# Edge filters as products over 32-row strips read back from memory, and image 0's first maxima ahead of the later filters

## The chip, the cores and the metric

One of the eight cores of a Trainium2 chip runs the whole program: TensorE (PE; PEld is its weight load), VectorE (DVE), ScalarE (ACT), GpSimd (POOL), and SyncE (SP), which issues most of the DMAs. The metric is the device time of one execution in microseconds.

## What is computed

A small two-layer "early fusion" model over eight images of 256 x 256 pixels and a text of 128 rows for each. The change concerns its first step only:

```python
w = (0.2989, 0.587, 0.114)
gray = einsum('bchw,c->bhw', x, w)                # x: 8 x 3 x 256 x 256, float32
edges = conv(gray, scharr, padding='SAME')        # two 3x3 filters
edge = abs(edges).sum(over the two filters) / 2   # 8 x 256 x 256
h = concat(edge, txt)                             # 8 x 384 x 256, 384 rows of 256 channels
```

Behind it stand layer 0 (normalisation, attention with 16 heads of 16 channels and two kinds of keys, whose softmaxes are mixed by alpha; then a feed-forward with blockwise 4-bit rounding) and layer 1 (attention over 64 anchors, then one shared and eight routed experts). All of it starts from `h`.

## The kernel before

All engines have instruction streams of their own, written out by hand, and wait on each other by semaphores. `attention0` holds the edge filters and layer 0's attention. Its attention runs as eight "turns", one an image (`for_images`, `turn`). A turn computes exponentials of scores of image i; beside them it prepares image i + 1's row maxima (`ring`) and image i + 2's projections. What the first turn needs has to be there before it: this part is the prologue, and the change lies in it wholly.

The prologue before, by engine:

- **SP** loads the pixels (`image(i)`, three DMAs of 256 KB, two buffers), weights, text, and the filters' taps. Then it stores the three bf16 parts of image 0's projections to DRAM (`store_parts(0)`, L374), reads them back as stacks of 16 partitions (`stacks`, L385; half 0 serves maxima 0 to 47, half 1 the rest), does the same for image 1 up to its first half, and writes the negated maxima of image 0 next to the queries (`maxima`, L394).
- **DVE** builds the filters' band matrices, makes gray rows of all eight images from the pixels (`make_gray`, L1083 and L1086), sums the two magnitudes into `h` (`edge_rows`, L1091), takes the moments of the three 128-row tiles of an image (`moments`, L1097, L1100), normalises images 0 and 1 (`inputs`, L939), computes the low parts of the projections (L950), and takes the 96 row maxima of image 0 (`ring`, L961) and their negation (L965, L968).
- **PE** computes the filters (`edges(i, n)`, L688, L692): a filter is three products with a banded 128 x 128 matrix over both 128-row halves of an image, 512 columns, and a fourth over six single rows that reach across the halves. Those rows are moved from partition to partition by two small DMAs an image, issued by ACT (`sides`, L860). Images 0 to 5 are filtered ahead of the ring, images 6 and 7 in pieces between its steps (`edge_piece`). PE also turns weights and inputs (L702, L550), projects (L559, L567) and makes the raw scores for the maxima (L588) in three PSUM banks; it can be three products ahead of DVE.
- **ACT** takes magnitudes (`magnitudes`, L843) and copies projections (L791).
- **POOL** makes masks and the third parts (`low_parts`, L507, L509).

The ring runs in 33 steps of three entries (`first_ring`), and the first eight also hold a piece of image 1's preparation (`PREPARE`: two transposes, six projections) in a single PSUM bank. The first score products of the first turn (L603) follow the last transpose of the maxima. A fp32 product is two records in the trace.

## Time and profile before

| | |
|---|---|
| time, median of three | 1818.8 us (1815.71 to 1819.44) |
| profiled execution | 1817.46 us |
| its span | 1815.7 us |
| mean granted clock of TensorE | 0.988 of full speed |
| busy: PE, PEld, DVE, ACT, POOL | 96%, 61%, 55%, 37%, 23% of the span |
| prologue | up to 138 us of the span |

The busy shares are averages over the whole span. Only the prologue bears on the change, and windows and timelines of it are what has to be read. TensorE counts as busy while it runs at half clock, and also while its pipelined products are spaced by waits, so PEclk has to be read beside it. "GB/s" is what the core's DMA rings moved; the rings are shared by all queues.

### The profile page before, as it was taken

To read this page: it belongs to the slowest core of one execution; us is meant where nothing else is said; L and a number is where in the kernel's file an instruction comes from. 1 tells how busy PE (TensorE), PEld (TensorE's weight loads), DVE (VectorE), ACT (ScalarE), POOL (GpSimd) and SP (SyncE) were. 2 spreads that over 40 slices of the span, in tenths; PEclk is the share of its full clock that TensorE was granted. 3 is DMA by queue.
4 is the path that set the end of the run, shared out by engine and by line. 5 is a ranking of instruction groups with operands and counts; after the bars stand their busy time and mean duration, and the time that the engine had idled before them with its cause. 6 is when DMAs were issued, how large, how long until landed. Compare 5 with 4: busy or idle time off the path is not lost.

```text
span 1815.7 us, 29086 instructions
## 1 busy us (share of the span) xinstructions
PE 1747.6 (96%) x9935; PEld 1115.4 (61%) x9935; DVE 1005.1 (55%) x2073; ACT 677.3 (37%) x1290; POOL 409.7 (23%) x415
## 2 busy tenths in 40 slices
PE   7989999899999998999999999999999999999997
PEld 3324444344444435777755666666767679999997
DVE  6597877778788898888865444443211112222221
ACT  2106656566666686545532322233010111111110
POOL 2101120110201003898722221110211211000000
PEclk9988999999999999999999999999999999999999
DMA  6832632426324402000074000000000003423211
GB/s 190 138 66 41 119 78 43 82 45 114 74 47 87 82 2 74 1 0 0 1 294 110 0 0 0 1 1 1 34 28 20 32 20 111 175 104 107 102 32 34
DMA packets 111955, 112.84 MB, mean 62 GB/s; under 512 B 11455, under 2 KB 104433, under 8 KB 111858
## 3 DMA queue, kind: packets, MB, share of 16 engines
q1 hardware_dynamic: 98610, 83.21, 20.3%
q10 hardware_dynamic: 9600, 18.92, 2.9%
q0 software_dynamic: 3648, 9.46, 1.4%
q8 instruction: 55, 0.90, 0.2%
q14 instruction: 42, 0.34, 0.1%
HBM read 78.51 MB, written 32.93 MB: 61 GB/s over the span
## 4 chain that ended last, share of the span: by engine, by line
PE 88%; DVE 7%; issue 2%; ACT 2%; DMA 0%; DVEq 0%; POOL 0%; ACTq 0%; POOLq 0%
PE ps_e L2218 11%; PE ps_e L2151 9%; PE ps_a L614 8%; PE ps_a L588 7%; PE ps_m L1651 6%; PE ps_a L603 6%; PE ps_e L2227 5%; PE ps_m L1794 5%; PE ps_e L2160 5%; PE ps_m L1722 4%; PE ps_m L1752 4%; PE ps_a L559 4%; PE ps_m L1667 3%; DVE mx L961 3%; PE ps_a L688 2%
## 5 line engine op out<-in xcount | busy, mean ns | idle before, releaser
L961 DVE TENSOR_REDUCE mx<-ps_a 128x1 f32<-128x384 f32 x768 | 379.7, 550 | 52.2 <-PE ps_a L588 50.4
L820 ACT ACTIVATE prob<-ps_a 128x768 f32<-128x768 f32 (+1 forms) x512 | 305.7, 650 | 96.7 <-PE ps_a L603 95.7
L588 PE MATMUL ps_a<-w,qs 96*128 96x384 bf16 x768 | 242.1, 338 | 7.7 <-DVE mx L961 3.8
L603 PE MATMUL ps_a<-qs,w 100*128 100x384 bf16 x768 | 207.1, 331 | 5.5 <-issue 4.0
L2218 PEld LDWEIGHTS ps_e<-xTr,w 128*128 128x128 f32 x1792 | 206.0, 193 | 2.2 <-issue 0.8
L2218 PE MATMUL ps_e<-xTr,w 128*128 128x128 f32 x1792 | 206.3, 276 | 0.6 <-DVE xTr L2394 0.6
L588 PEld LDWEIGHTS ps_a<-w,qs 96*128 96x128 bf16 x768 | 72.9, 98 | 182.2 <-DVE mx L961 103.6
L614 PE MATMUL ps_a<-prob,vp 128*32 128x384 f32 x1536 | 163.3, 498 | 0.0
L2151 PE MATMUL ps_e<-xT_all,w 128*128 x448 | 145.7, 486 | 0.0
L2283 ACT ACTIVATE gel_r<-ps_e 128x512 f32<-128x512 f32 x56 | 33.4, 597 | 280.9 <-PE ps_e L2218 280.9
L1651 PE MATMUL ps_m<-w 128*128 128x352 f32 x384 | 122.3, 462 | 2.2 <-ACT w L1828 1.2
L2151 PEld LDWEIGHTS ps_e<-xT_all,w 128*128 128x128 f32 x448 | 85.0, 190 | 57.8
L603 PEld LDWEIGHTS ps_a<-qs,w 100*128 100x128 bf16 x768 | 71.2, 99 | 68.8 <-ACT prob L820 18.0
L2251 ACT ACTIVATE gel<-ps_e 128x384 f32<-128x384 f32 x64 | 31.4, 491 | 203.7 <-PE ps_e L2151 203.7
L2300 DVE TENSOR_TENSOR hid_e<-gel,ps_e 128x384 f32<-128x384 f32 x64 | 35.5, 555 | 129.7 <-ACT gel L2251 129.1
L2227 PE MATMUL ps_e<-w,hid_r 128*128 128x256 f32 x448 | 101.3, 379 | 0.0
L1605 POOL TENSOR_TENSOR attn<-lg,gsum 128x1024 f32<-128x1024 f32 x24 | 45.6, 1902 | 234.6 <-DVE gsum L1487 234.6
L2405 DVE TENSOR_TENSOR hid_r<-gel_r,ps_e 128x512 f32<-128x512 f32 x56 | 38.5, 688 | 102.1 <-ACT gel_r L2283 102.1
L1651 PEld LDWEIGHTS ps_m<-w 128*128 128x128 f32 x384 | 69.9, 190 | 37.7 <-DVE w L1395 2.2
L1722 PE MATMUL ps_m<-wsT,xT_a 128*128 128x512 f32 x192 | 87.1, 596 | 4.8 <-DVE lg L1478 4.8
L516 POOL TENSOR_TENSOR y<-y 128x192 f32<-128x192 f32 x32 | 21.4, 670 | 310.8 <-DVE y L987 310.8
L2133 POOL DMA_INDIRECT out_dram<-y_e,row_id x28 | 27.6, 986 | 278.5 <-DVE row_id L2411 278.5
(266 smaller groups left out, 2585.1 us busy)
## 6 DMA issues: line engine op xcount, KB each, us to landing
w<-parts_dram SPq DMA_DIRECT2D x192, 96.0 KB, 5.2
w<-in_L_ffn_W_dram ACTq DMA_DIRECT2D x18, 1024.0 KB, 8.3
parts_dram<-w SPq DMA_DIRECT2D x24, 576.0 KB, 3.4
qs<-parts_dram SPq DMA_DIRECT2D x96, 96.0 KB, 4.0
prob<-in_x_dram SPq DMA_DIRECT2D x24, 256.0 KB, 3.6
w<-in_L_ffn_W_dram SPq DMA_DIRECT2D x6, 1024.0 KB, 12.8
grouped_x<-empty_row SPq DMA_DIRECT2D x1, 4352.0 KB, 24.3
grouped_h<-empty_row SPq DMA_DIRECT2D x1, 4240.5 KB, 33.9
```

Source lines behind the costliest of these rows:

```text
L588: mm = pe.matmul(ps[:, r % 3, 0:T], qs[0:NS, b, u // 2, t * P:(t + 1) * P], ks[0:NS, b, u % 2, u // 2], start=True, stop=True)
L603: mm = pe.matmul(ps[:, scores_at(v, more) + t, 0:T], ks[0:NS + 4, b, kp, hh, t * P:(t + 1) * P], qs[0:NS + 4, b, hh], start=True, stop=True)
L614: mm = pe.matmul(ps[j * SLOT:(j + 1) * SLOT, 7, 0:T], vp[:, b, t, g // 2 * QUAD + j], prob[:, g % 2, j, t], start=(t == 0), stop=(t == TT ...
L820: act.activation(prob[:, g % 2, j, ts.start:ts.stop], ps[:, at + ts.start:at + ts.stop, 0:T], ACT.Exp).then_inc(exp_done.sem, 1)
L961: dve.tensor_reduce(at, ps[:, r % 3, 0:T], AX.X, ALU.max).then_inc(ring_free.sem, 1)
L1651: mm = pe.matmul(ps[:, 2 * (u % 2) + n, 0:HALF0], xT[:, t, k], wguT[:, n, k, s * HALF0:(s + 1) * HALF0], start=(k == 0), stop=(k == KC - 1))
L1722: mm = pe.matmul(ps[:, bank + n], xT1[:, k, t * P:(t + 1) * P], wsT[:, k, n * 512:(n + 1) * 512], start=(k == 0), stop=(k == KC - 1))
L1794: mm = pe.matmul(ps[:, 2 + t % 2, 0:C], attnT[:, a, t * P:(t + 1) * P], gs[:, a], start=(a == 0), stop=(a == PAIRS - 1))
L2151: mm = pe.matmul(ps[:, 2 * (a % 2) + m, 0:T], w12[:, 0, m, k, a * P:(a + 1) * P], xT_of(i)[:, k], start=(k == 0), stop=(k == KC - 1))
L2160: mm = pe.matmul(ps[:, 4 + t, 0:C], hid[:, a, t * P:(t + 1) * P], w3[:, 0, a], start=(a == 0), stop=(a == IT1 - 1))
L2218: mm = pe.matmul(ps[:, 2 * n + m, a * P:(a + 1) * P], w12[:, b, m, k, n * HALF1 + a * P:n * HALF1 + (a + 1) * P], xTr[:, k], start=(k == 0 ...
L2227: mm = pe.matmul(ps[:, 4, 0:C], hid_r[:, a], w3[:, b, a], start=(a == 0), stop=(a == IT1 - 1))
```

## The change

The filters work on strips. The gray rows of an image are stored to an internal DRAM buffer of 258 rows of 288 floats, with zeros around, and are read back by SP in eight strips of 32 output rows: for each of the three column shifts, the 32 rows, and in a separate DMA the two rows below, 3 x 34 = 102 partitions in all, 8 x 256 columns. A filter is then one product a strip, with a matrix of 102 x 32, four strips side by side in TensorE's column groups. The single-row DMAs of ACT, the corner matrix and the zeroing for them go.

The order changes too. Filters 0, 1 and 2 stand ahead of the ring, filters 3 to 7 in steps 6, 16, 20, 24 and 28 of it. The first turn of the weights comes ahead of filters 0. The second half of image 0's stacks, then `kinds(1)`, `store_parts(1)` and `stacks(1, 1, 0)`, stand behind more loads, stores and strips in SP's queue. GpSimd sums the magnitudes of images 2 to 7 (`edge_rows`) and, for images 4 to 7, the gray rows from pixels that ACT has scaled (`scale_gray`, `sum_gray`); DVE did both before. All moments stay on DVE, those of images 2 to 7 in steps 2, 9, 19, 23, 27 and 31. ACT loads its table by a square root at the start, and issues the six DMAs of the taps.

```diff
-    OFFS = (-1, 0, 1)
+    PAD = IMG + 32
+    gray_dram = nc.dram_tensor("gray_dram", [B, IMG + 2, PAD], F32, kind="Internal").ap()
...
+    STRIP = 32
+    HALO = 2
+    ROWS = 3 * (STRIP + HALO)
+    STRIPS = IMG // STRIP
+    SIDE = 16
+    BY_DVE = 4
+
+
+    CONV_AT = {6: 3, 16: 4, 20: 5, 24: 6, 28: 7}
+
+    def shifted_rows(kx):
+
+        return (kx * STRIP, 0, STRIP), (3 * STRIP + kx * HALO, STRIP, HALO)
...
+        im = in_prob(2, STRIPS, IMG).rearrange("p (u s n) -> p u s n", u=2, s=STRIPS)
...
+        grays = k1[:, 0:B * 2 * PAD].rearrange("p (i a n) -> p i a n", i=B, a=2)
+        zero_row = q1[0:B, 0:PAD]
...
-                if i >= 2:
+                if 2 <= i < 2 + BY_DVE:
                     sp.wait_ge(gray_step.sem, gray_step.at(i - 1, 0))
+                elif i >= 2:
+                    sp.wait_ge(summed.sem, summed.at(i - 1 - BY_DVE, 0))
                 for ch in range(3):
                     sp.dma_start(pix[:, i % 2, ch], x[i, ch].rearrange("(a p) c -> p a c", p=P)
                                  ).then_inc(pix_in[i % 2].sem, 16)
 
-            sp.dma_start(taps[:], scharr.rearrange("f o a b -> (f o a b)").partition_broadcast(P)
-                         .rearrange("p (f a b) -> p f a b", f=2, a=3)).then_inc(taps_in.sem, 16)
+            def store_gray(i):
+
+                if i < BY_DVE:
+                    sp.wait_ge(gray_step.sem, gray_step.at(i + 1, 0))
+                else:
+                    sp.wait_ge(summed.sem, summed.at(i + 1 - BY_DVE, 0))
+                sp.dma_start(gray_dram[i, 1:IMG + 1].rearrange("(a p) n -> p a n", p=P), grays[:, i]
+                             ).then_inc(gray_out[i % 2].sem, 16)
+
+            def strips(i):
+
+                sp.wait_ge(row_out.sem, 32)
+                sp.wait_ge(gray_out[i % 2].sem, gray_out[i % 2].at(i // 2 + 1, 0))
+                if i >= 2:
+                    sp.wait_ge(edges_done.sem, edges_done.at(i - 1, 0))
+                for kx in range(3):
+                    for to, first, count in shifted_rows(kx):
+                        corner = gray_dram[i, first:first + 1, SIDE - 1 + kx:SIDE + kx]
+                        rows = bass.AP(corner.tensor, corner.offset, [[PAD, count], [STRIP * PAD, STRIPS], [1, IMG]])
+                        sp.dma_start(im[to:to + count, i % 2], rows).then_inc(im_in[i % 2].sem, 16)
...
+            sp.wait_ge(row_zero.sem, 1)
+            for row in (0, IMG + 1):
+                sp.dma_start(gray_dram[:, row], zero_row).then_inc(row_out.sem, 16)
...
+            store_gray(0)
+            strips(0)
...
+            image(2)
+            store_gray(1)
+            image(3)
+            strips(1)
+            store_gray(2)
...
             sp.wait_ge(kinds_made.sem, 4)
             kinds(0)
+            strips(2)
+            store_gray(3)
             store_parts(0)
             stacks(0, 0, 0)
+            image(4)
+            strips(3)
+            image(5)
             stacks(0, 0, 1)
-
-            sp.wait_ge(edges_done.sem, edges_done.at(BESIDE, 0))
+            for i in range(4, B):
+                store_gray(i)
+                if i + 2 < B:
+                    image(i + 2)
+                strips(i)
+
             kinds(1)
...
+            def edge_rows(i):
+
+                pool.wait_ge(mag_done.sem, mag_done.at(i, 2))
+                pool.tensor_tensor(h[:, i * TT:i * TT + 2], mag[:, i % 2, 0], mag[:, i % 2, 1], ALU.add).then_inc(h_later.sem, 1)
+
+            def sum_gray(i):
+
+                j, g = i - BY_DVE, gray_of(i)
+                pool.wait_ge(scaled_done.sem, scaled_done.at(j, 2))
+                pool.wait_ge(borders.sem, 3)
+                pool.tensor_tensor(g, pix[:, i % 2, 0], pix[:, i % 2, 1], ALU.add).then_inc(summed.sem, 1)
+                pool.wait_ge(scaled_done.sem, scaled_done.at(j, 3))
+                pool.wait_ge(summed.sem, summed.at(j, 1))
+                pool.tensor_tensor(g, g, pix[:, i % 2, 2], ALU.add).then_inc(summed.sem, 1)
+
             for n in range(3 * KC):
                 low_parts(0, n)
+            edge_rows(2)
             for n in range(3 * KC):
                 low_parts(1, n)
+            sum_gray(4)
+            sum_gray(5)
+            edge_rows(3)
+            sum_gray(6)
+            edge_rows(4)
+            sum_gray(7)
+            for i in range(5, B):
+                edge_rows(i)
             for_images(pool, turn)
...
-            def edges(i, n):
-
-                u, (f, kx) = i % 2, TAPS[n]
-                gray, side = gray_of(i), side_of(i)
-                if n == 0:
-                    pe.wait_ge(gray_step.sem, gray_step.at(i, 3))
-                    if i >= 2:
-                        pe.wait_ge(mag_done.sem, mag_done.at(i - 1, 0))
-                if i == 0 and kx == 0:
-                    pe.wait_ge(bands_done.sem, 9 * (f + 1))
-                out = ps[:, 4 + 2 * u + f].rearrange("p (a c) -> p a c", a=2)
-                if kx < 3:
-                    mm = pe.matmul(out, band[:, f, kx], gray[:, :, kx:kx + IMG], start=(kx == 0), stop=False)
+            def edges(i):
+
+                u = i % 2
+                pe.wait_ge(im_in[u].sem, im_in[u].at(i // 2 + 1, 0))
+                if i >= 2:
+                    pe.wait_ge(mag_done.sem, mag_done.at(i - 1, 0))
                 else:
-                    if f == 0:
-                        pe.wait_ge(side_in[i].sem, 32)
-                    mm = pe.matmul(out, corner[:, f], side, start=False, stop=True)
-                if n == len(TAPS) - 1:
+                    pe.wait_ge(bands_done.sem, 6)
+                for f in range(2):
+                    for a in range(2):
+                        for c in range(STRIPS // 2):
+                            mm = pe.matmul(ps[c * STRIP:(c + 1) * STRIP, 4 + 2 * u + f, a * IMG:(a + 1) * IMG], band[0:ROWS, f],
+                                           im[0:ROWS, u, a * (STRIPS // 2) + c], start=True, stop=True, tile_position=(0, c * STRIP))
                     mm.then_inc(edges_done.sem, 1)
...
-            pe.wait_ge(corner_in.sem, 32)
-            for n in range(len(TAPS)):
-                edges(0, n)
             pe.wait_ge(ident_done.sem, 1)
             pe.wait_ge(w_in.sem, 80)
             for n in range(5):
                 turn_weight(n)
-            for n in range(len(TAPS)):
-                edges(1, n)
+            edges(0)
...
-            for i in range(2, BESIDE):
-                for n in range(len(TAPS)):
-                    edges(i, n)
+            edges(1)
+            edges(2)
             pe.wait_ge(rest_done.sem, rest_done.at(0, 3 * KC))
             pe.wait_ge(v_done.sem, v_done.at(0, 2))
             last = None
@@ -731,9 +785,8 @@
                 ring(0, 0, first_ring(r))
                 if r < len(PREPARE):
                     last = in_bank3(PREPARE[r][0], 1, PREPARE[r][1], last)
-                i, n = edge_piece(r)
-                if i is not None:
-                    edges(i, n)
+                if r in CONV_AT:
+                    edges(CONV_AT[r])
...
+            def scale_gray(i):
+
+                u = i % 2
+                act.wait_ge(pix_in[u].sem, pix_in[u].at(i // 2 + 1, 0))
+                for ch in range(3):
+                    act.mul(pix[:, u, ch], pix[:, u, ch], GRAY[ch]).then_inc(scaled_done.sem, 1)
...
+            for kx in range(3):
+                for to, _, count in shifted_rows(kx):
+                    act.dma_start(taps[to:to + count].rearrange("p f a -> p (f a)"),
+                                  scharr.rearrange("f o a b -> b (f o a)")[kx].partition_broadcast(count),
+                                  allow_slow_non_contiguous=True).then_inc(taps_in.sem, 16)
+            act.wait_ge(borders.sem, 1)
+            act.activation(rstd[:, 0:1], eps[:], ACT.Sqrt, bias=eps[:]).then_inc(root_done.sem, 1)
             for n in range(5):
                 act.wait_ge(wTd.sem, n + 1)
                 act.copy(wT[:, n].rearrange("p k c -> p (k c)"), ps[:, n % 4]).then_inc(wTe.sem, 1)
+            magnitudes(0)
+            act.wait_ge(root_done.sem, 1)
             roots(0, 1)
-            sides(2)
-            magnitudes(1)
             for k in range(KC):
                 copy_inputs(0, k, k)
-            high_part(0, 0, KC)
-            roots(1, 2)
-            for n in range(1, 3 * KC):
+            for n in range(3 * KC):
                 high_part(0, n, (KC + n) % 4)
-                if n < 5:
-                    sides(n + 2)
             for n in range(2):
                 copy_v(0, 0, n, (4 * KC + n) % 4)
-            sides(7)
-            for i in range(2, BESIDE):
+            magnitudes(1)
+            roots(1, 2)
+            magnitudes(2)
+            for step, n in PREPARE:
+                if step == "inputs":
+                    copy_inputs(1, n)
+                else:
+                    high_part(1, n)
+            scale_gray(4)
+            scale_gray(5)
+            magnitudes(3)
+            scale_gray(6)
+            magnitudes(4)
+            scale_gray(7)
+            for i in range(5, B):
                 magnitudes(i)
-            for r in range(FIRST):
-                if r < len(PREPARE):
-                    step, n = PREPARE[r]
-                    if step == "inputs":
-                        copy_inputs(1, n)
-                    else:
-                        high_part(1, n)
-                i = edges_before(r, 0)
-                if i is not None:
-                    magnitudes(i)
-                if edges_before(r, 4) == B - 1:
-                    roots(2, B)
-            act.wait_ge(h_edge.sem, h_edge.at(B, 0))
+            roots(2, B)
+            act.wait_ge(h_later.sem, h_later.at(B - 2, 0))
             for_images(act, turn)
...
+                if i < 2:
+                    dve.wait_ge(h_edge.sem, h_edge.at(i, 1))
+                else:
+                    dve.wait_ge(h_later.sem, h_later.at(i - 1, 0))
...
+            dve.wait_ge(taps_in.sem, 96)
+            dve.wait_ge(masks_done.sem, 17)
             n = 0
             for f in range(2):
-                for kx in range(3):
-                    def tap(ky):
-                        return taps[:, f, ky, kx:kx + 1]
-                    main = band[:, f, kx]
-                    dve.tensor_scalar(main, masks[:, 0], tap(0), None, ALU.mult).then_inc(bands_done.sem, 1)
+                to = band[0:ROWS, f]
+                dve.tensor_scalar(to, masks[0:ROWS, 0], taps[0:ROWS, f, 0:1], None, ALU.mult).then_inc(bands_done.sem, 1)
+                n += 1
+                for ky in (1, 2):
+                    dve.wait_ge(bands_done.sem, n)
+                    dve.scalar_tensor_tensor(to, masks[0:ROWS, ky], taps[0:ROWS, f, ky:ky + 1], to, ALU.mult, ALU.add
+                                             ).then_inc(bands_done.sem, 1)
                     n += 1
-                    for ky in (1, 2):
-                        dve.wait_ge(bands_done.sem, n)
-                        dve.scalar_tensor_tensor(main, masks[:, ky], tap(ky), main, ALU.mult, ALU.add
-                                                 ).then_inc(bands_done.sem, 1)
-                        n += 1
-                if f == 0:
-                    dve.wait_ge(borders.sem, 3)
-                    make_gray(0)
-            make_gray(1)
-            dve.memset(side_rows[0][0][:, 2 * SW:], 0.0).then_inc(side_zero.sem, 1)
-            dve.memset(side_rows[1][0], 0.0).then_inc(side_zero.sem, 1)
-            make_gray(2)
-            dve.wait_ge(alpha_in.sem, 16)
-            dve.tensor_scalar(al[:, 1:2], al[:, 0:1], -1.0, 1.0, ALU.mult, ALU.add).then_inc(bands_done.sem, 1)
+            dve.wait_ge(borders.sem, 3)
+            make_gray(0)
             edge_rows(0)
             dve.wait_ge(text_in.sem, 16)
             moments(0)
             inverses(0, 0, 1)
             inputs(0)
-            make_gray(3)
-            edge_rows(1)
-            moments(1)
-            make_gray(4)
+            make_gray(1)
+            make_gray(2)
             for n in range(3 * KC):
                 low_parts(0, n, (KC + n) % 4)
-                if n in (1, 3):
-                    make_gray(5 + n // 2)
+                if n == 3:
+                    make_gray(3)
+            edge_rows(1)
+            dve.wait_ge(alpha_in.sem, 16)
+            dve.tensor_scalar(al[:, 1:2], al[:, 0:1], -1.0, 1.0, ALU.mult, ALU.add).then_inc(bands_done.sem, 1)
+            moments(1)
             inverses(1, 1, 2)
             inputs(1)
-            make_gray(7)
-            for i in range(2, BESIDE - 1):
-                edge_rows(i)
-                moments(i)
             dve.wait_ge(borders.sem, 4)
-            dve.wait_ge(bands_done.sem, 19)
+            dve.wait_ge(bands_done.sem, 7)
+            MOMENTS_AT = {2: 2, **{r + 3: i for r, i in CONV_AT.items()}}
             for r in range(FIRST + 1):
                 ring(0, first_ring(r))
                 if r < len(PREPARE) and PREPARE[r][0] == "project":
                     low_parts(1, PREPARE[r][1])
-                if r == 2:
-                    edge_rows(BESIDE - 1)
-                if r == 3:
-                    moments(BESIDE - 1)
-                i = edges_before(r, 2)
-                if i is not None:
-                    edge_rows(i)
-                    moments(i)
+                if r in MOMENTS_AT:
+                    moments(MOMENTS_AT[r])
```

## Rows read from the trace of the kernel before

**Rows 1.** The page, part 6: DMA issues, KB each, median us to landing.

```profile
parts_dram<-w SPq DMA_DIRECT2D x24, 576.0 KB, 3.4
...
prob<-in_x_dram SPq DMA_DIRECT2D x24, 256.0 KB, 3.6
```

**Rows 2.** Windows by stage: PE, PEld, DVE, ACT, POOL busy, PEclk, DMA share, GB/s.

```profile
45.70:76.20 30.50, 30.50 (x65) 10.66 (x63) 10.57 (x30) 4.50 (x9) 3.31 (x5) 1.00 1.04 171
97.30:138.10 40.80, 34.89 (x103) 11.23 (x103) 38.53 (x89) 2.48 (x5) 1.42 (x2) 0.85 0.39 59
```

**Rows 3.** Timeline of PE: start us, us, engine line, op, count.

```profile
15.24 1.12 PE L692 MATMUL ps_a<-qs,prob 6*128 6x512 f32 x2 [1.37 <-DMA qs<-w]
...
45.72 2.74 PE L688 MATMUL ps_a<-w,prob 128*128 128x512 f32 x6
...
75.15 1.12 PE L692 MATMUL ps_a<-qs,prob 6*128 6x512 f32 x2
76.20 0.66 PE L588 MATMUL ps_a<-w,qs 96*128 96x384 bf16 x3
...
138.07 0.80 PE L603 MATMUL ps_a<-qs,w 100*128 100x384 bf16 x2
```

**Rows 4.** Timeline of PE in the first turn: the weighted sum with V.

```profile
150.88 0.85 PE L614 MATMUL ps_a<-prob,vp 128*32 128x384 f32 x8
151.67 0.34 PE L588 MATMUL ps_a<-w,qs 96*128 96x384 bf16 x1
```

**Rows 5.** Timeline of DVE: start us, us, engine line, op, count.

```profile
7.24 1.42 DVE L1086 SCALAR_TENSOR_TENSOR w<-prob,w 128x512 f32<-128x512 f32 x2
...
27.29 1.06 DVE L939 TENSOR_SCALAR w<-h,mv,rstd 128x256 f32<-128x256 f32 x3
...
97.34 5.81 DVE L961 TENSOR_REDUCE mx<-ps_a 128x1 f32<-128x384 f32 x12
...
112.78 0.68 DVE L1091 TENSOR_TENSOR h<-prob 128x512 f32<-128x512 f32 x1
113.49 1.08 DVE L1097 BATCH_NORM_STATS2 bn<-h 128x6 f32<-128x256 f32 x3
...
114.70 2.85 DVE L961 TENSOR_REDUCE mx<-ps_a 128x1 f32<-128x384 f32 x6
...
138.55 0.28 DVE L968 SCALAR_TENSOR_TENSOR mneg<-ps_a,mneg 48x128 bf16<-48x128 f32 x1
```

**Rows 6.** Timeline of ACT: issue of two of the DMAs of single rows.

```profile
25.82 1.38 ACTq L860 DMA_DIRECT2D qs<-w  x2
```

**Rows 7.** Timeline of SP: DMA issues, start us, us, line, count.

```profile
43.42 1.57 SPq L450 DMA_DIRECT2D w<-kind_rows  x2
45.03 6.49 SPq L374 DMA_DIRECT2D parts_dram<-w  x3
...
60.86 2.79 SPq L385 DMA_DIRECT2D qs<-parts_dram  x6
...
99.52 3.35 SPq L385 DMA_DIRECT2D qs<-parts_dram  x6
```

**Rows 8.** Windows: clock and DMA at five points, columns as in rows 2.

```profile
18.00:19.50 1.50, 1.50 (x3) 0.47 (x3) 1.10 (x2) 0.00 (x0) 0.00 (x0) 0.50 0.02 7
100.00:102.00 2.00, 1.97 (x9) 0.67 (x7) 1.94 (x5) 0.00 (x0) 0.00 (x0) 1.00 1.05 350
104.00:106.00 2.00, 1.93 (x7) 0.66 (x6) 2.00 (x6) 0.00 (x0) 0.00 (x0) 1.00 1.15 129
114.00:116.00 2.00, 0.70 (x3) 0.19 (x2) 2.00 (x8) 0.00 (x0) 0.00 (x0) 1.00 0.06 10
130.00:132.00 2.00, 2.00 (x5) 0.41 (x4) 2.00 (x5) 0.00 (x0) 0.00 (x0) 0.50 0.00 0
```

**Rows 9.** Groups of instructions by form, POOL: sums of 256 and 768 columns.

```profile
L1567 POOL TENSOR_TENSOR w<-w 128x256 f32<-128x256 f32 x22 | 16.0, 728 | 4.6 <-ACT w L1847 4.6
...
L1613 POOL TENSOR_TENSOR h<-h,bo 128x768 f32 x6 | 10.9, 1819 | 0.0
```

More of the change, by code:

```diff
@@ L261, in attention0 @@
         kind_rows = sb("kind_rows", [4, KINDS, T], BF16)
-        taps = sb("taps", [P, 2, 3, 3])
+        taps = sb("taps", [P, 2, 3])
+        band = sb("band", [P, 2, STRIP])
+        masks = sb("masks", [P, 3, STRIP])
         ps = ctx.enter_context(nc.psum_tensor("ps_a0", [P, 8, 512], F32))
```

90 lines of the change are left out of this document (31 added, 59 removed).

## The prediction

> **What bounds the kernel now.** I read the stage windows first. The change touches only what stands ahead of the first attention turn, whose first score product starts at 138.07 [rows 3]; no instruction behind it is edited, so all that the change can do is to move that point, and the rest with it. Inside this prologue the windows [rows 2] show who is the bound. From 45.7 to 76.2 TensorE is busy all 30.5 us. The timeline of PE says with what: filter products of images 2 to 5, 64 records from 45.72 to the one at 75.15, 7.6 us an image [rows 3]. Right behind them, at 76.20, comes the first "ring" product (maxima of image 0's raw scores), and it did not wait for its operands. The next 21.1 us, up to 97.34 [rows 3, 5], are eight steps of three maxima with a projection, a round trip PE, ACT, DVE each. From 97.3 to 138.1 DVE is the bound, 38.5 us busy of 40.8 [rows 2]: twelve maxima take 5.81 us, 0.485 each [rows 5].
>
> **What the filters cost after.** Removed are 64 products of 512 columns, 8 x 7.6 = 61 us of PE. In their place stand 16 products of 256 columns an image, in four column groups. The nearest row is the weighted sum with V, four products in four column groups, 384 columns, 8 records: 0.79 us from its start to the next [rows 4]. 256 columns give 0.53, taken as 0.55: 2.2 us an image at full clock, about 4.2 at half. One after the other it would be some four times that; the row shows that they don't run so.
>
> **The front of the new schedule.** The taps are now six DMAs on ACT at 0.69 us of issue [rows 6], from 0.8 to 4.9; with 3.6 us to landing [rows 1] they are there at 8.5, after the pixels. Six small band operations follow, estimated at 0.23 us (9.9), then the gray rows of image 0, whose last two operations take 1.42 [rows 5], 1.9 in all (11.8). Then a round trip through memory that before did not exist: a store, 3.4 us to landing [rows 1] (15.2), and six strip DMAs. These carry 0.82 MB. Bounds of their rate: 350 GB/s, as the stores of 768-byte rows show, and 129, as the loads into 16 partitions show [rows 8]: 2.3 to 6.3 us. I take 250, between them, 3.3 us; with issue and landing 5.5: 20.7. TensorE has idled, so its clock is low, and filters 0 end at 24.9. Then ACT's second magnitude 0.55, sum 0.71, moments 1.21, root and inverse 0.55, normalising 1.1 [rows 5]: 29.0. Before, that was done at 28.35, but the transposes stood behind image 1's filters on PE, until 31.6. The projections begin some 2 us earlier, and ACT and DVE no longer hold them up with other images: the low parts are ready at about 45.
>
> **SP's queue** decides what that is worth. Gray 1 is ready at 30.9. Store to landing 3.4, strips(1) 2.8 (six issues, [rows 7]), store of gray 2 0.4, kinds 1.6, then gray 2's landing at 40.5, strips(2) 2.8, store of gray 3: SP reaches the stores of the parts at 43.7. (Before it came at 45.03, but waited for the parts until 51.5 [rows 7].) In the DMA rings lie strips(2) until 44.4, gray 3 until 45.2, the parts' 1.77 MB at 350 GB/s until 50.3. The first half of the stacks then needs 13 us: for image 1 it was issued from 99.52 [rows 7], and the rings were busy from 100 to just before 114 [rows 8]. So the ring can begin at 63.3 instead of 76.2; call this point R. The strips' bounds, which count twice, give R = 61.3 to 69.3. Before, the same half would have been there at about 65, and the filters hid it. Images 4 and 5 and strips(3), 2.4 MB, now stand ahead of the second half, which so comes some 20 us after R; the ring wants it 41 us after R: hidden.
>
> Here a rule of the Trainium skill speaks against the change: SBUF — State Buffer, Door 1: The DMA port swizzle, states that 32 partitions reach 8 of the 16 ports, and 16 partitions 4. The trace agrees for 16 partitions, 129 GB/s against 350 [rows 8]. By it the strips would run at half of 350, 4.7 us each, and R would be 66.1.
>
> **The ring after.** DVE's own work from R on: 96 maxima x 0.485 = 46.6; two negations with what they wait for 1.7; six low parts 3.3; moments of six images at 1.21 = 7.3 (before three images with their sums, 1.92 each, 5.8 [rows 5]). That is 58.9. Its waits:
> The first eight steps took 21.1 us. Now filters 3 stand in step 6 (2.2 us, of which the round trip's slack takes 0.6), and TensorE starts cold after 15 us with little work (1.5 for two projections at half clock): 24.2, of which 8.1 is idle.
> In step 9 DVE waits for the moments of image 3, whose sum is now GpSimd's, behind four more sums (gray 4 and 5). GpSimd gets the last low part at R + 24.2 and needs 1.5 for it. A sum of 512 columns lies between 0.73 (256) and 1.82 (768) [rows 9]: 1.27. Five of them are 6.4: R + 32.0. DVE is there at R + 27.1. Wait 4.9.
> Filters 4 to 7 stand in steps 16, 20, 24, 28. PE is at most three products ahead of DVE, 1.1 us of cover once its last is made. Its clock: with nothing but maxima in its queue it was 0.50 at 130 to 132, though PE counts as busy, and with filters between the maxima (100 to 102) 1.00 [rows 8]. Here the maxima stand alone between bursts, behind a wait of 4.9 us. I take half clock and 4.0 us a burst. The first costs 4.0 + 0.3 - 1.1 = 3.2; the other three, beside which DVE has moments, 2.1 each: 9.5.
> Sum 58.9 + 8.1 + 4.9 + 9.5 = 81.4; the last negation ends at 63.3 + 81.4 = 144.7. Before it was 138.8 [rows 5]. **Later by 5.9 us.**
> SP once more: strips(7) go at R + 56 (filters 5 done), then kinds, three stores, the stacks of image 1, and only then the first half of the negated maxima, which the first turn waits for. By the same prices (2.8 + 1.6 + 1.2, landing 3.4, stacks 13) and 1 for the last: R + 79. Hidden by 2.4 us, no more. ACT's DMAs of single rows and DVE's zeroing, which go, lay beside PE's work, and the table load moved to the start lies beside transfers: nothing. The strips of images 3 to 6 are there 4 us or more before their step: nothing.
>
> The rule on the clock in the Trainium skill, TensorE: Matmul & The Clock Gate, Part 1: The HAM clock gate, is that low is the default and sustained activity lifts it. The rows agree for the maxima alone; what it makes of short bursts no row here shows.
>
> **The rivals.**
> - Faster: the clock stays high. Then filters 0 take 2.2 (R earlier by 2.0), the cold start goes (1.5), the first burst costs 1.3 and the others 0.3 (7.3 less): 10.8 less, 133.9, or 1813. It is faster once more than 5.9 of these are saved, so it needs the bursts and more than them. For it: with 2.0 us of filters in 4 the clock was 1.00 [rows 8]. Against it: at 18.0 to 19.5 it was 0.50, behind a pause of TensorE of 1.37 us, up to 15.24, only [rows 3, 8]. 0.16.
> - No change that can be told: only the bursts run at full clock (7.3 less, 137.4, 1816), or the strips come at 350 GB/s and half of the bursts' excess goes (1818). 0.28.
> - DMA becomes the bound: strips at 129 GB/s. R moves to 69.3, and the chain of strips(7), stores and stacks grows by 3, to R + 82, and takes DVE's place: first turn at 151.5 or later, 1830 to 1831. Against it: 1 KB rows and twice the partitions. 0.18.
> - My forecast 0.38; its own range 1820 to 1828.
>
> **Numbers.** The profiled execution took 1817.5, its span is 1815.7; the median shown is 1818.8, 1.3 more. 1817.5 + 5.9 = 1823.4; with half of the 1.3 I give 1824. The range reaches from next to the fast rival (1813) to beyond the DMA one: 1814 to 1834. A measurement of this kernel tells 0.2%, 3.6 us. Faster is the first rival, 0.16; same the second, 0.28; slower the rest, 0.56.
>
> **What would show it.** The ring's first product (96x384) at 60 to 69; a filter burst of 16 products near 2.2 or 4.2 us; PEclk near 0.5 in the 50 us before the first turn; DVE idle by 5 us ahead of image 3's moments, released by GpSimd; DVE idle 2 to 3 us behind the bursts; strips landing in 4 to 7 us. The prediction is wrong if the ring starts before 60, if the bursts don't stop DVE, or if SP's stacks of image 1 come after the ring's end.

## The result and the profile after

The changed kernel takes 1828.85 us in the median (1827.89 to 1830.47) against 1817.97 for the kernel before in the same session: 1.0064 times as long, 95% interval [1.005, 1.0079]. It is slower by 10.9 us. The forecast was 1824 against 1818.8, a ratio of 1.003, within 1814 to 1834. The profiled execution's span is 1828.2 us, 12.5 longer than before's 1815.7; it is of the longest of the four executions, 1830.47. "The ring" is the one of the maxima, "the rings" are those of the DMA engines. The rows below are of that one execution, and so is every comparison of single points with [rows 2 to 7].

Timeline of TensorE after; columns as in [rows 3]: start, length, instruction, count, and in brackets the idle time ahead of it with what ended it.

```profile
15.37 1.09 PE L761 MATMUL ps_a<-ident,osb 128*128 128x128 f32 x4 [15.37 <-DMA w<-in_L_attn_W_O_dram]
27.28 3.61 PE L751 MATMUL ps_a<-prob,band 102*32 102x256 f32 x32 [7.41 <-DMA prob<-gray_dram]
...
49.78 1.93 PE L751 MATMUL ps_a<-prob,band 102*32 102x256 f32 x32
57.20 3.64 PE L751 MATMUL ps_a<-prob,band 102*32 102x256 f32 x32 [5.48 <-DMA prob<-gray_dram]
72.60 1.12 PE L652 MATMUL ps_a<-w,qs 96*128 96x384 bf16 x3 [11.77 <-DMA w<-parts_dram]
...
90.24 1.93 PE L751 MATMUL ps_a<-prob,band 102*32 102x256 f32 x32
...
113.46 3.64 PE L751 MATMUL ps_a<-prob,band 102*32 102x256 f32 x32
122.57 3.64 PE L751 MATMUL ps_a<-prob,band 102*32 102x256 f32 x32
...
131.34 3.64 PE L751 MATMUL ps_a<-prob,band 102*32 102x256 f32 x32
140.21 3.47 PE L751 MATMUL ps_a<-prob,band 102*32 102x256 f32 x32
...
153.29 0.80 PE L667 MATMUL ps_a<-qs,w 100*128 100x384 bf16 x2 [2.89 <-DMA qs<-mneg]
```

An image's filters took 7.6 us before [rows 3]; now they are one burst (L751) of 1.9 or 3.6. But TensorE stands idle for 7.4, 5.5 and 11.8 us, each time until a DMA lands, and the ring (L652) begins at 72.6, only 3.6 us earlier than before, although the filters ahead of it have gone from 45 us (six images) to 9. The last row is the first turn's first product: 153.3 after, 138.1 before. So the prologue loses 15.2 us. From that product to the end of the span it is 1674.9 us, before 1677.6: 2.7 less. Only 0.6 of it lies in the first turn (from its first product to ACT's first copy of `vp` 9.96 us against 10.54), 0.9 between the third and the fourth turn's first such copy and the rest behind the last of them, in parts that are the same in both kernels. There one execution differs from the next anyway: in one session spans of the kernel before reach from 1811.6 to 1820.0.

Timeline of VectorE in the ring: maxima L1014, moments L1153, negation L1018 and L1021.

```profile
95.09 2.87 DVE L1014 TENSOR_REDUCE mx<-ps_a 128x1 f32<-128x384 f32 x6
103.34 1.08 DVE L1153 BATCH_NORM_STATS2 bn<-h 128x6 f32<-128x256 f32 x3 [5.38 <-POOL h L569]
...
117.52 0.28 DVE L1018 TENSOR_SCALAR mneg<-ps_a 48x128 bf16<-48x128 f32 x1 [3.15 <-PE ps_a L650]
...
126.58 4.27 DVE L1014 TENSOR_REDUCE mx<-ps_a 128x1 f32<-128x384 f32 x9 [1.92 <-PE ps_a L652]
...
135.45 4.27 DVE L1014 TENSOR_REDUCE mx<-ps_a 128x1 f32<-128x384 f32 x9 [2.03 <-PE ps_a L652]
...
143.98 4.27 DVE L1014 TENSOR_REDUCE mx<-ps_a 128x1 f32<-128x384 f32 x9 [1.69 <-PE ps_a L652]
...
150.75 0.28 DVE L1021 SCALAR_TENSOR_TENSOR mneg<-ps_a,mneg 48x128 bf16<-48x128 f32 x1
```

The wait for GpSimd in step 9 is 5.38 us, and the four half-clock bursts stop DVE for 3.15, 1.92, 2.03 and 1.69: 8.8. The last negation ends at 151.0, 78.4 us behind the ring's start; before it was 62.6 [rows 3, 5].

SyncE's queue. L438 stores gray rows, L451 issues strips, L369 stores parts, L380 reads the stacks, L389 writes negated maxima.

```profile
6.46 2.56 SPq L458 DMA_DIRECT2D w<-in_L_attn_W_V_dram  x1
...
15.32 0.37 SPq L438 DMA_DIRECT2D gray_dram<-w  x1
18.93 2.10 SPq L451 DMA_DIRECT2D prob<-gray_dram  x6
...
39.47 2.08 SPq L451 DMA_DIRECT2D prob<-gray_dram  x6
41.60 0.38 SPq L438 DMA_DIRECT2D gray_dram<-w  x1
...
49.78 2.07 SPq L451 DMA_DIRECT2D prob<-gray_dram  x6
...
52.32 4.12 SPq L369 DMA_DIRECT2D parts_dram<-w  x3
59.20 2.69 SPq L380 DMA_DIRECT2D qs<-parts_dram  x6
...
130.13 4.48 SPq L369 DMA_DIRECT2D parts_dram<-w  x3
138.02 2.69 SPq L380 DMA_DIRECT2D qs<-parts_dram  x6
140.76 5.63 SPq L380 DMA_DIRECT2D w<-parts_dram  x12
146.44 7.65 SPq L389 DMA_DIRECT2D qs<-mneg  x8
```

SP waits for each landing before it can go on: 3.2 us for gray 0, but 7.8 for gray 2 (from the issue's end, 41.98, to 49.78), 2.8 from the last part store to the stacks, and 3.4 at the end. The first negated maxima, finished at about 118.1, are issued at 146.4.

Windows, columns as in [rows 2]; the last three numbers are PEclk, DMA share and GB/s.

```profile
4.00:6.00 2.00, 0.00 (x0) 0.00 (x0) 0.00 (x0) 0.87 (x2) 1.50 (x9) 1.00 0.61 196
6.00:8.00 2.00, 0.00 (x0) 0.00 (x0) 0.00 (x0) 0.00 (x0) 1.94 (x5) 1.00 0.41 118
8.00:10.00 2.00, 0.00 (x0) 0.00 (x0) 0.00 (x0) 0.00 (x0) 0.79 (x2) 1.00 0.49 144
10.00:12.00 2.00, 0.00 (x0) 0.00 (x0) 0.04 (x1) 0.00 (x0) 0.00 (x0) 1.00 0.93 263
...
20.00:24.00 4.00, 0.00 (x0) 0.00 (x0) 0.00 (x0) 0.49 (x1) 0.00 (x0) 0.99 1.02 217
39.50:49.80 10.30, 10.30 (x37) 6.38 (x35) 6.12 (x9) 3.53 (x7) 6.40 (x9) 0.93 0.80 192
113.50:117.10 3.60, 3.60 (x34) 1.39 (x34) 0.86 (x2) 0.60 (x1) 0.00 (x0) 0.50 1.02 215
```

At 6 to 10 us, with 1.3 MB of weights and 1 MB of text to load, the rings move only 118 to 144 GB/s, where the kernel before moved 342 and 287. While strips load (20 to 24) they are full at 217. While gray 2's store lies in them (39.5 to 49.8) they move 192. In the burst of 113.5 TensorE counts as busy throughout, at a granted clock of 0.50, the lower of its two levels.

### The profile page after: what moved, and what is told of

Same layout as the page of the kernel before. It is cut to its first block, busy times and chain, and to the rows that moved or that the text cites. A ratio compares the mean times of both kernels' runs of the same rounds, so it can differ in the third digit from the quotient of the medians.

```text
span 1828.2 us, 29414 instructions
## 1 busy us (share of the span) xinstructions
PE 1717.6 (94%) x10063; PEld 1104.6 (60%) x10063; DVE 984.9 (54%) x2039; ACT 684.1 (37%) x1302; POOL 427.6 (23%) x442
## 4 chain that ended last, share of the span: by engine, by line
PE 83%; DVE 6%; DMA 3%; issue 3%; ACT 2%; SPq 1%; POOL 1%; DVEq 0%; ACTq 0%; POOLq 0%
PE ps_e L2254 11%; PE ps_e L2187 9%; PE ps_a L678 7%; PE ps_a L652 6%; PE ps_m L1687 6%; PE ps_a L667 6%; PE ps_e L2263 5%; PE ps_e L2196 5%; PE ps_m L1830 5%; PE ps_m L1758 4%; PE ps_m L1788 4%; PE ps_m L1703 3%; PE ps_a L623 3%; DVE mx L1014 2%; PE ps_m L1768 1%
## 5 line engine op out<-in xcount | busy, mean ns | idle before, releaser
L1014 DVE TENSOR_REDUCE mx<-ps_a 128x1 f32<-128x384 f32 x768 | 379.3, 549 | 71.9 <-PE ps_a L652 70.3
L652 PE MATMUL ps_a<-w,qs 96*128 96x384 bf16 x768 | 248.2, 346 | 24.8 <-DMA w<-parts_dram 11.8
L652 PEld LDWEIGHTS ps_a<-w,qs 96*128 96x128 bf16 x768 | 73.4, 98 | 198.6 <-DVE mx L1014 105.4
L1641 POOL TENSOR_TENSOR attn<-lg,gsum 128x1024 f32<-128x1024 f32 x24 | 45.6, 1901 | 234.7 <-DVE gsum L1523 234.7
```

The source lines that it names most:

```text
L652: mm = pe.matmul(ps[:, r % 3, 0:T], qs[0:NS, b, u // 2, t * P:(t + 1) * P], ks[0:NS, b, u % 2, u // 2], start=True, stop=True)
L1014: dve.tensor_reduce(at, ps[:, r % 3, 0:T], AX.X, ALU.max).then_inc(ring_free.sem, 1)
```

## The experiments

Ratios are to the kernel before on the same chip, five rounds each. A landing moves by 2 to 3 us from one execution to the next: the ring's start was 66.7, 70.0 and 68.6 in three kernels whose schedule up to there is the same. So a ratio decides, and a single point only where it moves by more. Most intervals are plus or minus 0.15%, 2.7 us, so two ratios are apart for certain only from some 0.2% on. Against the changed kernel's 1.0064 that holds for experiments 2 (barely), 8, 10 and 12; where a smaller step is read (3 us in experiment 4, 2 in experiment 7), it rests on the wait that the trace shows.

**1. Gray 0 without the taps.** In DVE's queue `make_gray(0)` goes ahead of the wait for the taps:

```diff
+            make_gray(0)
             dve.wait_ge(taps_in.sem, 96)
...
-            make_gray(0)
```

> Against the changed kernel (ratio 1.0064; ring from 72.6, its last negation at 151.0, first turn at 153.3). Theory A, DVE's order is what holds the first gray rows (they stand behind the bands, which wait for the taps until 12.0): gray 0 is stored some 5 us earlier, strips 0 land that much earlier, the ring begins at 68 and the time falls by 5 us, ratio 1.0037. Theory B, the rings themselves are clogged by the taps' small reads, and 2.3 MB of weights and text stand ahead of the store in any order: the store lands at 17.5 to 18 instead of 18.9, time down by 0 to 1.4 us, ratio 1.0056 to 1.0064.

Ratio 1.0064 [1.0048, 1.0079], no change. The rows were stored 3.3 us earlier, at 12.01, and landed at 18.81 instead of 18.93; the ring began at 72.8. The store only lay longer in the rings. That DVE waited for the taps was not what held up the front, the rings were: the second theory.

**2. Taps in one transfer.** The six DMAs, which pick single floats of `scharr`, become one of 18 contiguous floats to each of 128 partitions; a product with a mask and a sum over three choose each partition's column on DVE.

```diff
-            for kx in range(3):
-                for to, _, count in shifted_rows(kx):
-                    act.dma_start(taps[to:to + count]..., "b (f o a)")[kx]...)
+            act.dma_start(all_taps[:], scharr...partition_broadcast(P)...)
```

> The taps come in one DMA of 18 floats a partition, as in the kernel before, and DVE picks the column of each partition group by a product and a sum. Theory B (the 612 reads of four bytes clog the rings: 56 to 196 GB/s in the first 10 us): pixels, weights and text land some 5 us earlier, gray 0 is stored by 10 and landed by 14, strips 0 land at 22 instead of 27, ring from 67, time down by 5 to 6 us, ratio about 1.0035. If the low rate has another cause, only the bands come earlier: gray 0 stored at 10, landed at 17 to 18, time down by 1 to 2 us.

1.0042 [1.0027, 1.0056], 4 us less by the ratios; span 1822.7, 5.5 less, but of the fastest of its six executions. Windows of this kernel:

```profile
4.00:6.00 2.00, 0.00 (x0) 0.00 (x0) 0.00 (x0) 0.00 (x0) 1.45 (x9) 1.00 1.08 355
6.00:8.00 2.00, 0.00 (x0) 0.00 (x0) 1.23 (x6) 0.00 (x0) 1.66 (x7) 1.00 0.99 302
```

Where the rings moved 196 and 118 GB/s, they now move 355 and 302. SP's two issues of weights that took 2.27 and 2.56 us take 0.46 and 0.47, all weights are in at 10.9 instead of 15.4, and gray 0, stored at 12.3 (expected by 10), lands 2.3 us behind its store. The stores of the zero rows, which are new too, are still there, so they were not the cause. The ring begins at 66.7, the first turn at 146.4, 6.9 us earlier. This is the clearest single cost in the front, and one that my prediction didn't have.

**3. Image 3 ahead of gray 4 and 5.** On ACT `magnitudes(3)` goes ahead of `scale_gray(4)` and `(5)`, on GpSimd `edge_rows(3)` ahead of their sums.

```diff
-            sum_gray(4)
-            sum_gray(5)
             edge_rows(3)
+            sum_gray(4)
+            sum_gray(5)
```

> Image 3's magnitudes and their sum stand ahead of the gray rows of images 4 and 5 on ACT and GpSimd. The wait of DVE in step 9 (5.4 us) goes. Theory A, DVE's queue is the bound up to the first turn: last negation at 146, and SP's last strips come as much earlier, so the time falls by 4 to 5 us, ratio 1.004. Theory B, SP's chain of strips, stores and stacks is the bound and is held by landings, not by DVE: first turn at 152 or later, time down by 0 to 1 us; the gray rows come 1.3 us later and the strips 4 may be late for step 16.

1.0069 [1.0055, 1.0083], no gain, with the step 9 wait gone and the last negation at 146.2 instead of 151.0. The rows that say why, TensorE and then SP:

```profile
108.54 3.64 PE L751 MATMUL ps_a<-prob,band 102*32 102x256 f32 x32 [2.51 <-DMA prob<-gray_dram]
...
153.88 0.80 PE L667 MATMUL ps_a<-qs,w 100*128 100x384 bf16 x2 [8.28 <-DMA qs<-mneg]
```

```profile
129.61 4.47 SPq L369 DMA_DIRECT2D parts_dram<-w  x3
145.85 6.22 SPq L389 DMA_DIRECT2D qs<-mneg  x8
```

The first turn waits 8.3 us for negated maxima: SP issues them at 145.9, in the changed kernel at 146.4. DVE's 5.4 us were off the path once SP's chain was the last to end: the second theory.

**4. The last parts' stores early.** In SP's queue `store_parts(1)`, with its wait, goes ahead of the loop over images 4 to 7.

```diff
             stacks(0, 0, 1)
+            for m in range(3):
+                sp.wait_ge(stack_in[1][m].sem, stack_in[1][m].at(1, 0))
+            store_parts(1)
             for i in range(4, B):
```

> The stores of image 1's parts go ahead of the loop over images 4 to 7 in SP's queue, nothing else. Theory A, SP's chain at the end (store, landing 7.9 us, stacks, negated maxima) holds the first turn by the 2.3 us between the last negation and the first score product: the negated maxima go at 118 to 139 and the first turn begins at 150.4, time down by 2 to 3 us, ratio 1.005. Rival: 1.8 MB more ahead of strips 4 make these late for step 16 (needed at 113.5), which gives back 0 to 3 us: no change.

1.0048 [1.0033, 1.0062]; span 1824.7, 3.5 less. The negated maxima are issued from 141.9, and the first turn's product (150.41) follows the last transpose (150.10) without a wait. So the chain was not hidden, and its wait cost some 3 us. Strips 4 were not late.

**5. Both orders, 3 and 4.**

> Both edits at once: image 3's sum ahead of the gray rows of 4 and 5, and the stores of image 1's parts ahead of the loop over images 4 to 7. Theory: the wait in step 9 is worth its 5.4 us only once SP's chain is out of the way. Last negation at 146 to 148 (strips 4 some us late for step 16), first turn right behind it, ratio 1.0025 to 1.0035. If the two edits only add up (0 and 3 us), ratio 1.0048.

1.0046 [1.0031, 1.0062]. The two together give what experiment 4 gives alone, and not the 1.0025 to 1.0035 of the theory: the last negation ends at 151.5, where 146 to 148 was expected. The wait moved:

```profile
113.86 3.64 PE L751 MATMUL ps_a<-prob,band 102*32 102x256 f32 x32 [4.04 <-DMA prob<-gray_dram]
```

Gray 4, summed later, is stored and read back later, and DVE waits 7.26 us behind this burst (3.15 before). Whatever is first in GpSimd's queue, the other is late, and the first turn still waits 1.4 us for the negated maxima.

**6. A filled TensorE.** The kernel of experiment 5, and from step 8 on a product of 512 fp32 columns whose result nobody reads, in each step without filters.

```diff
                 if r in CONV_AT:
                     edges(CONV_AT[r])
+                elif r >= len(PREPARE):
+                    ...
+                    pe.matmul(ps[:, 3], ident[:], wT[:, 0]..., start=True, stop=True)
```

> e5_sum_and_store and, from step 8 on, in each step without filters one product of 512 columns whose result nothing reads, in the free fourth bank, the load that the filter pieces were in the kernel before. Theory A, half clock is what makes a burst cost DVE 2 to 3 us: PEclk 1.00 up to the end of the ring, a burst takes 1.93 instead of 3.64, DVE's waits behind the four bursts fall from 8.8 to 2, of which strips 4, late by then, take back 3: ratio 0.002 below e5_sum_and_store. Theory B, the bursts' length in PE's queue doesn't matter since strips come late anyway: same ratio as e5_sum_and_store within 0.0005.

1.0053 [1.0036, 1.007], as in experiment 5. Here are its bursts and its first turn:

```profile
111.16 2.31 PE L751 MATMUL ps_a<-prob,band 102*32 102x256 f32 x32 [2.91 <-DMA prob<-gray_dram]
119.56 1.93 PE L751 MATMUL ps_a<-prob,band 102*32 102x256 f32 x32
127.10 1.94 PE L751 MATMUL ps_a<-prob,band 102*32 102x256 f32 x32 [0.48 <-DMA prob<-gray_dram]
136.19 3.41 PE L751 MATMUL ps_a<-prob,band 102*32 102x256 f32 x32 [2.02 <-DMA prob<-gray_dram]
...
149.87 0.58 PE L667 MATMUL ps_a<-qs,w 100*128 100x384 bf16 x2 [2.51 <-DMA qs<-mneg]
```

Busier between the bursts, TensorE keeps the full clock and a burst takes 1.93 us (the first, behind a wait of 2.9, 2.31; the last, behind one of 2.0, 3.41), so the half clock was due to the maxima standing alone. But now the bursts wait for their strips, the first turn for the negated maxima, and the time doesn't change: the full clock buys nothing while transfers end last. The filling has a small price of its own (21 maxima take DVE 10.28 us instead of 9.81), less than the 1.7 us per burst that the clock gives back.

**7. No round trip.** The strips read the red plane of the pixels and don't wait for stored gray rows, which are still stored; the filters so work on red alone.

```diff
-                sp.wait_ge(gray_out[i % 2].sem, gray_out[i % 2].at(i // 2 + 1, 0))
...
-                        corner = gray_dram[i, first:first + 1, SIDE - 1 + kx:SIDE + kx]
+                        corner = x[i, 0, first:first + 1, kx:kx + 1]
```

> The strips are read from the red plane of the input instead of from the stored gray rows and don't wait for the store (the filters then work on other data; stores and all bytes moved stay). Theory, the round trip store, landing, strips holds the front: strips 0 land at 19 instead of 27, the ring begins at 62 to 66, strips 4 to 7 are never waited for and SP's last chain starts earlier; time down by 7 to 10 us, ratio 1.001 to 1.0025. Rival, the volume of the DMA rings is the bound: landing orders change but the ring begins at 70 or later, time down by 3 us or less.

1.005 [1.0034, 1.0065]: the rival, not the 7 to 10 us of the theory. Filters 0 started 2.1 us earlier (25.17) and the ring 2.2 (70.39), where the store and its landing, now out of the strips' way, had been 3.6 us (15.32 to 18.93). At 18 to 25 the rings are full at 225 to 269 GB/s, and strips 0 took 9.4 us from issue to first product, 8.35 in the changed kernel: what they share the rings with sets when they land. The round trip as such is worth some 2 us of the 10.9, and its ratio alone doesn't tell that apart from nothing.

**8. The kernel before with one more image beside the ring.** Nothing of the strips; `BESIDE` is 5, so the pieces between the ring's steps are those of images 5 to 7. The last roots are taken once, behind all magnitudes.

```diff
-    BESIDE = 6
+    BESIDE = 5
+        late_sides = sb("late_sides", [6, (B - BESIDE) * 2 * IMG])
```

> The kernel before with one edit of the order: the filters of images 5, 6 and 7, not only 6 and 7, in pieces beside the ring's steps 8 to 31. Theory, the order is the good half of the change and the trip through memory the bad one: the ring begins at 68.6 instead of 76.2 (its stacks are there at 66), the ring takes as long as before, and the first turn begins at 131; sum and moments of image 7 now stand behind the ring, which gives back up to 2 us. Ratio 0.996 to 0.9975. Rival: the stacks land later than the ring could start, or steps 24 to 31 get longer: ratio 0.999 or above.

1814.14 us, ratio 0.9979 [0.9968, 0.999]: faster than both kernels. Timeline of TensorE:

```profile
66.77 0.66 PE L589 MATMUL ps_a<-w,qs 96*128 96x384 bf16 x3
...
129.94 0.52 PE L604 MATMUL ps_a<-qs,w 100*128 100x384 bf16 x2 [0.25 <-issue]
```

The ring begins at 66.8 without waiting (76.2 before), and the first turn follows 63.2 us later (61.9 before), since TensorE has room beside DVE's maxima. So the first turn begins 8.1 us earlier, and it gives 2.4 of them back: TensorE waits 3.05 us for ACT's first exponentials, 0.63 before, since image 7's moments, the roots and a table load now stand ahead of them. The profiled execution was the fastest of its twelve, so its 7.4 us of span are more than the 3.8 that the ratio gives. The ratio lies between the two that were expected (up to 0.9975, from 0.999). The idea of the ring ahead of later filters is good; it needed no strips.

**9 and 10. Combinations.** Taps in one transfer with early stores (2 and 4), and all four edits (2 to 4 and the filling).

> Two edits to the changed kernel: the taps come as one contiguous transfer and are selected by a product and a sum, and the stores of the last parts stand ahead of the transfers of images 4 to 7 in SP's queue. Theory A (the front and SP's last chain are separate costs, so that they add): the ring's first score product at 66 to 68 (66.7 with the taps alone), last negation 78 us behind it, at 144 to 146, first turn right behind it; first turn 7 to 9 us earlier than in the changed kernel (153.3), ratio to the kernel before 1.001 to 1.003. Theory B (the earlier stores fill the rings for the strips, which come earlier too, so that one of the two is all there is): first turn at 146 to 148, ratio 1.004.

> Four edits together: taps as one transfer, image 3's magnitudes and sum ahead of those of gray 4 and 5, early stores of the last parts, and an unread product of 512 columns in each ring step from 8 on without filters. Theory A (each wait removed shortens the way to the first turn once the others are gone): ring at 66 to 68, no wait for GpSimd in step 9, bursts about 2 us at full clock, first turn at 141 to 144, ratio 0.999 to 1.002. Theory B (behind the front the transfers are the bound, so sum and filling add nothing to taps and early stores): first turn at 144 to 147 and the ratio within 0.1% of that of taps and stores alone; waits for strips on PE in place of the removed ones.

Experiment 9 gives 1.0046 [1.0031, 1.0062] with a span of 1824.5, experiment 10 1.004 [1.0026, 1.0054] with 1822.5. The savings don't add, though the ring of experiment 9 also had a late start (70.0, with the taps alone 66.7). First turns at 147.3 and 145.6 fit the second theory each time. In experiment 10 PE waits 3.0 us for the strips of image 4 and 3.0 for those of image 7, where DVE then stands for 5.0:

```profile
107.17 2.72 PE L760 MATMUL ps_a<-prob,band 102*32 102x256 f32 x32 [2.96 <-DMA prob<-gray_dram]
...
132.66 3.64 PE L760 MATMUL ps_a<-prob,band 102*32 102x256 f32 x32 [3.04 <-DMA prob<-gray_dram]
```

**11 and 12. Image 3 later.** Its load goes behind `strips(2)`, its gray rows behind image 0's last low part, their store behind the first stacks; alone, and with 2 and 4.

```diff
-            image(3)
             strips(1)
...
             strips(2)
+            image(3)
-            store_gray(3)
             store_parts(0)
             stacks(0, 0, 0)
+            store_gray(3)
```

> The changed kernel with image 3's load behind strips(2) instead of ahead of strips(1), its gray rows made after the last low part of image 0 instead of between them (3.1 us of VectorE, from 45.7), and their store behind the first stacks. Theory A (image 3's 0.8 MB ahead of gray 2's store, and its gray rows between the low parts, hold up the start of the ring): gray 2 lands within 5 us instead of 8, the parts are complete by 49.5 instead of 52.4, the ring starts at 67 to 69.5 instead of 72.6; the first turn 2 to 4 us earlier, ratio 1.003 to 1.005. Theory B (all that image 3's load held up is held up by it later, since it must pass before filters 3): the ring at 71.5 to 73.5 and the ratio unchanged, 1.006 to 1.007.

> The same edit together with the taps as one transfer and the early stores of the last parts. Theory A (the front's two delays add): ring at 61 to 65, first turn at 139 to 142, ratio 0.999 to 1.002. Theory B (behind the front the strips and parts of the later images bound the ring phase, so that an earlier ring only waits more): the ring at 61 to 65 too, but PE waits for strips in steps 6 or 16 and the first turn comes at 143 to 147, ratio 1.003 to 1.005.

Alone 1.0063 [1.0047, 1.0079]: nothing, the second theory. Gray 2 still took 6.0 us to land, behind the strips of image 1 themselves, and the ring began at 71.9. Nor were the parts complete by 49.5: without gray 3 between them GpSimd is the bound, the last five of its six low parts, 1.44 us each, stand back to back, and it ends at 51.1. With both others 1.003 [1.0017, 1.0043], the ring at 67.5 instead of the 61 to 65 of both theories, the first turn at 144.7: the best of this schedule, still slower than before. Ratio and first turn are those of the second theory, but its reason is not: no burst in the ring waits for strips, and the first turn waits for no DMA.

## Why the prediction came out right, and where its sizes were off

The direction was right, and the time lies in the range, 5 us above its middle; but that range was 20 us wide, and the forecast's own, 1820 to 1828, was missed by 0.9. The reason was right in kind: the prologue goes from TensorE's work to transfers and waits, and loses. The sizes were less so. R is the start of the ring:

- **The start of the ring**: 63.3 forecast, 69.3 as its upper bound, measured 72.6. This is the term that was mis-sized, by 9.3 us. *The taps* were put at 3.6 us to landing; they landed at 11.96, 8.7 behind their last issue, and gray 0 was done at 15.3 instead of 11.8. Experiment 2 shows that the taps' six DMAs held up everything in the rings, experiment 1 that DVE's wait for them cost nothing more. *Strips 0* took 8.35 us from issue to their first product instead of 5.5: the rate (217 GB/s, forecast 250) was nearly right, but two images are issued right behind and share the rings. By the Trainium skill, SBUF — State Buffer, Door 1, 32 partitions would give half of 350. The trace doesn't agree for the six DMAs of an image together: from 120.5 to 121.7 the rings hold strips(6) alone and move 255 GB/s, next to the 250 that I took. (For 16 partitions the prediction called 129 against 350 an agreement; it is 0.37, and 4 of 16 ports would be a quarter.) No run has one such DMA alone. *Gray 2* took 8.2 us from issue to landing instead of 3.4. *The parts* were complete at 52.4 instead of about 45. I had priced each landing by a row with quieter rings, and not asked what makes the parts last: gray 3's 3.1 us between DVE's low parts, and GpSimd's 1.44 us for each (experiment 11). In SP's queue this adds up so: it reached the stores of the parts at 52.3, forecast 43.7, and from there to the ring it took 20.3 us, forecast 19.6.
- **Filters on strips**: 2.2 and 4.2 us forecast, 1.93 and 3.64 measured. The row of the V sum was the right neighbour: groups run side by side.
- **First eight steps**: 24.2 forecast, 22.5 measured. **Step 9**: wait 4.9 forecast, 5.4 measured; GpSimd's sum of 512 columns 1.27 forecast, 1.26 measured. **Bursts at half clock**: 9.5 forecast, 8.8 measured. The whole ring phase: 81.4 against 78.4. Its price was right, but experiments 3 and 6 correct what I read into it: taking the step 9 wait or the half clock away gains nothing, since strips and SP's chain are ready no sooner. Each of these waits covered another; in the schedule of experiment 12, where from the ring's start on nothing waits for a transfer, this was not tried.
- **SP's last chain**: forecast to land at R + 79, "hidden by 2.4 us, no more"; it landed at 153.3, R + 80.7, and the first turn waited 2.9 us for it. Strips(7) went earlier than forecast (R + 53.9 against R + 56), but the three stores took 4.5 us to issue instead of 1.2, and from the stacks' first issue to the landing it was 15.3 instead of 14. Experiment 4 gets 3 us of it back.
- **The sum**: the ring starts 9.3 later than forecast, its phase is 3.0 shorter, the chain adds 3.0 between the last negation and the first turn (138.8 to 138.1 before, 151.0 to 153.3 after), and what lies behind is 2.7 shorter, mostly not by the change: 5.9 + 9.3 - 3.0 + 3.0 - 2.7 = 12.5, the difference of the spans. The errors partly cancelled, and that the time stayed inside the range by 5 us is in part luck.
- **Rivals**: what came is nearest to the third, at 0.18: DMA becomes the bound, R is 69.3 or later, SP's chain takes DVE's place, first turn from 151.5 on, 1830 to 1831. Measured were 72.6, 153.3 and 1828.85. But its cause, strips at 129 GB/s, was not the one. The forecast's own signs were missed at two places: the ring's first product at 60 to 69 (72.6), and strips landing in 4 to 7 us (8.35). "The clock stays high" is refuted by PEclk 0.50 in the bursts. That it would gain as much as I had worked out is refuted too, for the ring's part of it (experiment 6). In the Trainium skill, TensorE: Matmul & The Clock Gate, Part 1: The HAM clock gate, sustained activity lifts the clock; experiment 6 agrees, with 1.93 us a burst once work stands between them. Whether that is worth time is for the other rows to say.

**Where 61 us of TensorE went.** Ahead of the ring 45.6 us of filters became 9.2, but the ring starts only 3.6 us earlier, since image 0's way through memory (gray rows, strips, parts, stacks) ends at 72.6, however little TensorE has to do. In the kernel before that way was shorter: with one image more beside it the ring began at 66.8 without waiting (experiment 8). The other 15 us had lain beside DVE's maxima, where TensorE had room. The best combination (experiment 12) leaves 0.3%: its ring starts 8.7 us earlier than before (67.5) and takes 15.4 longer (78.0 from start to last negation, 62.6 before), with the waits of 5.4 in step 9 and 8.9 behind the bursts still in it. How that loss divides among them is open, and neither this schedule without these waits nor one that transfers less was tried.

## What to carry to other kernels

A filter that is cheaper on TensorE is no gain where the next bound is a chain of transfers: first work out when that chain would be ready without the filters, with the rings as full as the new schedule makes them. Price a landing by what lies in the rings when it is issued, since one priced at 3.4 us took 8.2 here. Where several waits end within a few us of each other, take them away together in the estimate: against the changed kernel's 0.64% the single edits left 0.42 (taps), 0.69 (sum first) and 0.48 (early stores), and all with the filling still 0.40. And try the change of order alone first; here moving one image beside the ring gained 0.2%.

## What the hardware showed that I had not expected

Six small DMAs (six single floats to each of 102 partitions, 612 in all, a few KB) held the rings at 118 to 196 GB/s for some 6 us and stalled another queue's issues to 2.6 us each; as one contiguous transfer the same stretch ran at 290 to 355. The Trainium skill, DMA: Bandwidth & Descriptors, Rules for kernel authors, has it that a non-contiguous last dimension becomes one descriptor an element. The trace agrees: in the first 14 us ACT's queue has 666 packets, and 144 with the single transfer. That this also slows the large loads of another queue is what experiment 2 adds. How it does is open: the 666 packets took only 2.2% of the engines' time, and from 4 to 10 us the engines were busy for 0.41 to 0.61 of it. And the rest of the program is not constant: 1674 to 1678 us from the first turn's first product to the end in these kernels, though hardly an edit touches what lies there, so a prologue that ends 1 us earlier doesn't always shorten the span by 1.
